# A fused graph kernel on Trainium2: the quotient of the mixing branch formed as 1 - eps/(v + eps)

## What is computed

```python
xn = _layernorm(x)
x = x + gnn(xn, edge_index) + mix(xn)      # graph attention, 8 heads of 32; mixing branch
x = x + ffn(_layernorm(x))                 # 8 gated experts, dense
```

```python
q = jax.nn.relu(q); k = jax.nn.relu(k)
vk  = jnp.einsum('ngdl,ngel->ngde', v, k)
out = jnp.einsum('ngde,ngdl->ngdl', vk, q)          # v * sum(k) * q here
out = out / (jnp.sum(v, -1, keepdims=True) + ATT_EPS)   # v itself here
```

## Time and profile before

| what | us |
|---|---|
| timed runs | 1016.85, 1018.16, 1018.79 |
| median | 1018.16 |
| profiled execution, span | 1012.8 |
| VectorE busy | 799.5 (79%) |
| TensorE busy | 911.4 (90%) |
| ScalarE busy | 589.4 (58%) |
| GpSimd busy | 377.3 (37%) |
| chain that ended last | TensorE 41%, GpSimd 34%, issue 13%, VectorE 7%, ScalarE 3%, DMA 2% |

### The profile page before, as it was taken

How to read it: one execution, slowest core, us unless ns; L and a number is a source line. 1 busy time by engine, 2 the same in 40 slices (tenths; PEclk the granted TensorE clock), 3 DMA queues, 4 the chain that set the end, 5 groups by cost and what they waited for, 6 DMA issues and landing times.

```text
span 1012.8 us, 14669 instructions
## 1 busy us (share of the span) xinstructions
PE 911.4 (90%) x4984; PEld 790.1 (78%) x4984; DVE 799.5 (79%) x1517; ACT 589.4 (58%) x1206; POOL 377.3 (37%) x408
## 2 busy tenths in 40 slices
PE   6897899989888999898746689999999999999997
PEld 5686788878777778777535578999988889898986
DVE  6778799988888888988786788775565778786867
ACT  4730456655656556666254566667665767666663
POOL 0167777777777777777773000000000000000000
PEclk9988899999999999998868799999999999999999
DMA  8434454454444444445563002000000010100013
GB/s 260 151 91 138 141 140 129 134 141 141 125 139 139 123 140 138 128 138 140 165 194 100 6 17 63 29 2 32 1 9 24 1 32 1 32 1 1 1 37 91
DMA packets 50362, 89.00 MB, mean 88 GB/s; under 512 B 9733, under 2 KB 33337, under 8 KB 50268
## 3 DMA queue, kind: packets, MB, share of 16 engines
q0 software_dynamic: 18768, 52.88, 19.0%
q1 hardware_dynamic: 30780, 34.66, 11.2%
q10 hardware_dynamic: 719, 0.27, 0.1%
HBM read 81.10 MB, written 6.68 MB: 87 GB/s over the span
## 4 chain that ended last, share of the span: by engine, by line
PE 41%; POOL 34%; issue 13%; DVE 7%; ACT 3%; DMA 2%; SPq 0%; POOLq 0%; DVEq 0%; ACTq 0%
POOL G L491 34%; PE bank L1043 9%; PE bank L1045 9%; PE bank L1044 9%; PE bank L1107 2%; PE bank L1110 2%; PE bank L837 2%; DMA x_in<-in_x 1%; PE bank L1108 1%; PE bank L1109 1%; PE bank L916 1%; ACT hid L741 1%; PE bank L872 1%; ACT sums L718 1%; PE bank L830 1%
## 5 line engine op out<-in xcount | busy, mean ns | idle before, releaser
L491 POOL DMA_INDIRECT G<-projected_rows,src_l x391 | 374.5, 958 | 166.6 <-issue 118.3
L741 ACT ACTIVATE hid<-bank,faff 128x512 f32<-128x512 f32 (+2 forms) x224 | 157.7, 723 | 111.1 <-PE bank L1045 109.3
L916 PE MATMUL bank<-G,oh 128*128 128x264 f32 x782 | 188.6, 400 | 21.3 <-DVE G L1422 21.1
L916 PEld LDWEIGHTS bank<-G,oh 128*128 128x128 f32 x782 | 153.5, 198 | 49.9 <-DVE G L1422 22.7
L1422 DVE TENSOR_TENSOR G<-G,bank 128x3072 f32<-128x3072 f32 (+1 forms) x33 | 109.1, 3306 | 0.0
L1716 DVE TENSOR_TENSOR hil<-hid,hil 128x1024 fp32r<-128x1024 f32 (+2 forms) x56 | 60.8, 1086 | 48.3 <-ACT hil L749 48.3
L1043 PE MATMUL bank<-frh,ew 128*128 128x512 f32 (+3 forms) x228 | 84.3, 370 | 4.4 <-DVE frl L1691 4.4
L1044 PE MATMUL bank<-frl,ew 128*128 128x512 f32 (+3 forms) x228 | 82.8, 363 | 0.0
L1045 PE MATMUL bank<-frh,ew 128*128 128x512 f32 (+3 forms) x228 | 82.8, 363 | 0.0
L1043 PE MATMUL bank<-hil,ew 128*128 128x512 f32 (+2 forms) x224 | 81.6, 364 | 0.0
L1045 PE MATMUL bank<-hil,ew 128*128 128x512 f32 (+2 forms) x224 | 81.2, 362 | 0.0
(11 more groups left out here) (344 smaller groups left out, 2059.3 us busy)
## 6 DMA issues: line engine op xcount, KB each, us to landing
dstb<-targets SPq DMA_DIRECT2D x32, 384.0 KB, 3.7
G<-projected_rows,src_l POOLq DMA_INDIRECT x391, 2.8
projected_rows<-sums SPq DMA_DIRECT2D x25, 132.0 KB, 2.2
x_in<-in_x SPq DMA_DIRECT2D x3, 1024.0 KB, 9.6
out<-feat_rows SPq DMA_DIRECT2D x23, 128.0 KB, 2.2
U<-in_x SPq DMA_DIRECT2D x4, 512.0 KB, 6.0
TT<-in_W SPq DMA_DIRECT2D x8, 256.0 KB, 3.3
wqkv<-in_W SPq DMA_DIRECT2D x8, 256.0 KB, 3.9
```

Source lines behind the costliest of these rows:

```text
L491: g.indirect_dma_start(out=G[slot][:, c, :], out_offset=None, in_=table[:, :], in_offset=bass.IndirectOffsetOnAxis(ap=src_l[:, grp, c:c + ...
L741: A.activation(hid[layer][:, m, 0:cols], bank[2 * layer + m][:, 0:cols], ACT.Relu, bias=faff[:, 2 * layer + 1, j:j + 1], scale=faff[:, 2 * ...
L916: ins = T.matmul(b_seg[g % 2][:, 0:ROW], oh[g % 2][:, c, :], G[g % SLOTS][:, c, :], start=(c == 0), stop=(c == ch - 1))
```

## The change

`ratio` forms v / (v + eps) as 1 - sign * (eps / |v + eps|). ScalarE gives eps / |v + eps| directly: ln(eps) is computed into a third column of `epsr` and is the bias of the exponential. VectorE keeps two instructions. `b_v` is no longer written.

```diff
-        epsr = [sb(f"epsr{i}", [P, 2]) for i in range(2)]
+        epsr = [sb(f"epsr{i}", [P, 4]) for i in range(2)]
...
                 chain.link(A.activation(e[:, 1:2], e[:, 0:1], ACT.Exp, scale=0.5, bias=lneps[:, 0:1]))
+                A.activation(e[:, 2:3], e[:, 1:2], ACT.Ln)
                 chain.link(A.activation(vbuf[t % 2], b_v[:, :], ACT.Abs, bias=e[:, 1:2]))
                 chain.link(A.activation(b_k[:, :], vbuf[t % 2], ACT.Ln))
-                A.activation(b_k[:, :], b_k[:, :], ACT.Exp, scale=-1.0)
+                A.activation(b_k[:, :], b_k[:, :], ACT.Exp, scale=-1.0, bias=e[:, 2:3])
...
                 par = t % 2
-                y = b_k[:, :]
                 dve.wait_ge(s["eps_ready"], t + 1)
-                link(V.tensor_tensor(b_v[:, :], b_v[:, :], kbuf[par], ALU.mult))
-                link(V.tensor_tensor(vbuf[par], vbuf[par], y, ALU.mult))
-                link(V.scalar_tensor_tensor(out=vbuf[par], in0=vbuf[par], scalar=-2.0, in1=y, op0=ALU.add, op1=ALU.mult))
-                link(V.tensor_tensor(b_v[:, :], vbuf[par], b_v[:, :], ALU.mult))
-                V.scalar_tensor_tensor(out=qbuf[par], in0=b_v[:, :], scalar=-1.0, in1=qbuf[par], op0=ALU.mult, op1=ALU.mult).then_inc(s["o_ready"], 1)
+                link(V.scalar_tensor_tensor(out=vbuf[par], in0=kbuf[par], scalar=-1.0, in1=b_k[:, :], op0=ALU.mult, op1=ALU.mult))
+                V.scalar_tensor_tensor(out=qbuf[par], in0=vbuf[par], scalar=1.0, in1=qbuf[par], op0=ALU.add, op1=ALU.mult).then_inc(s["o_ready"], 1)
```

## The result

| | before | after |
|---|---|---|
| timed runs, median of 8 each | 1017.69 us (1015.02 to 1018.79) | 1021.1 us (1019.17 to 1021.59) |
| ratio | | 1.0037, 95% interval [1.0026, 1.0048] |
| profiled execution, span | 1012.8 | 1018.5 |
| VectorE busy | 799.5 | 747.7 |
| gathers, busy (391) | 374.5 | 378.8 |

The change takes 52 us of work off VectorE and makes the kernel 3.4 us slower, by the medians. The prediction was 1021.4 (1018.16 + 3.3); the median of before has moved to 1017.69 with five more runs.

The account below looks back on a forecast made before the run. GpSimd's unpaused gathers were taken as the bound, so VectorE's saving counts nothing. Gathers held in 21 tiles at 0.157 us add 3.3 us to 1018.16, giving 1021.4 us, range 1017.2 to 1024.8.

Parts of the forecast that it names:

- The bound: From 133 to 485 us GpSimd's unpaused gathers set the time; VectorE's saved 49 us become waiting, 18.6 to about 68 us.
- VectorE's two instructions: In `ratio`, per tile: 0.72 us for the first with its link, 0.69 for the second, 1.41 instead of 3.59.
- ScalarE's 0.20 us: Ahead of VectorE's pair in each tile: added Ln 0.11 us, exponential's bias 0.09; VectorE starts 0.20 us later.
- The hold: A gather starting under the second, two-SBUF-input instruction lengthens by that instruction's end past its start less 0.125 us: about 0.16 us.
- The sum: Over 25 tiles, 21 held gathers at mean 0.157 us add 3.3 us to 1018.16, giving 1021.4 us.
- the one-hot excess: Gathers lengthened under one-input L1354: all such excess about 1 us in 133 to 485 us, its change taken as 0.
- 1 (the phase misses): In the tiles the second instruction ends too early to hold gathers much: 1018.2 to 1020.1 us, about 1019.6; 22%.
- 2 (only L1354's kind holds a gather): Two-SBUF-input instructions hold no gather; every gather under the new instruction keeps 0.95 us: 1018.2 us; 8%.
- 3 (VectorE paces the stage): VectorE, not GpSimd, bounds the tile stage, so its 49 us saving shows in the time: 969 us; 1%.
- 4 (a better clock at the end of the gathers): Group 31's sums and the dense stage's start run at a higher clock: 1016 us with no or little hold; 5%.
- 5 (a worse phase by ScalarE's part): ScalarE adds 0.33 us per tile, raising the hold to 6.0 us: 1024.2 us; 64% together with the forecast.
- 5.4 us between a span and a time: Whole kernel: the timed median lies 5.4 us above the profiled span, a distance kept for the forecast span of 1016.1 us.

Follow-up runs that it names:

- the second experiment: The changed kernel with one tiny linked VectorE instruction between the pair, so the second instruction runs 0.19 us later: 1.0069 of before, 1024.6 us.
- experiment 11: The changed kernel measured once more, unaltered, beside the kernel before: 1.0032 of before, 1020.89 us.
- Experiment 3: The changed kernel with three tiny linked VectorE instructions between the pair, so the second instruction runs 0.57 us later: 1.0024 of before, 1018.6 us.
- experiments 1, 4 and 5: 1: changed kernel, pair's intermediate result in PSUM, 1.0014 of before; 4: kernel before, L1546 with both inputs from SBUF, 1.0041; 5: kernel before, L1547 likewise, 1.0002.

## Why the prediction was right, point by point

- **The bound.** Gathers on GpSimd, with VectorE waiting for them: right. VectorE lost 52 us of work, and its wait rose to 69.2 us, "about 68" in the prediction.
- **VectorE's two instructions.** 0.72 to the second's start and 0.69 for it; measured 274.40 - 273.68 = 0.72, and 0.69. The working for the second was circular: its slope of 1 ns a column was drawn through L1544's own 687 ns, so it had to come out at 0.69. It assumed that both forms cost the same, and they do.
- **ScalarE's 0.20 us.** The Ln 0.11, as estimated; the bias 0.08 (0.58 us for this exponential before, 0.66 after). VectorE's wait for Sign rose from 0.18 to 0.36, so 0.18 in all.
- **The hold.** 0.29 us of overlap past the start expected, 0.25 to 0.29 measured in 22 tiles; 0.16 us each expected, 0.12 to 0.16 measured. The formula (end past the start, less 0.125 us), read from three rows, held in all of them: 0.28 past the start at 274.81 gives 0.16, and the gather has 1.10. It held at other phases too: 0.58 to 0.59 in the first tile (0.46; the gather has 1.41), 0.44 in the second experiment (0.32; it has 1.26).
- **The sum.** 21 tiles and 3.3 us expected; 23 tiles and 3.7 us in the trace, 3.4 us in the time. The first tile had 0.46, where the largest term expected was 0.26. The gathers' total rose by 4.3, since the one-hot excess rose by 0.6 as well, which the prediction had put at 0. It had taken all excess of the kernel before in 133 to 485 us for about 1 us, and the trace has 1.7. That the forecast of 1021.4 lies only 0.3 us from the measured median is partly luck: the median of before moved by 0.5 us, and by the ratio the loss is 3.8 us here and 3.3 in experiment 11.
- **The rivals.** 1 (the phase misses) did not come: two tiles missed, not all. Experiment 3 made it happen, and 1.0024 was left, the 2 us that are open. 2 (only L1354's kind holds a gather) is refuted by experiments 1, 4 and 5. This was also what the inference in the Trainium skill ("SBUF — State Buffer", section "Who interferes with whom") came to; it does not hold for these gathers, the fourth experiment's tensor_tensor being the plainest case. The first half of that rule, that a two-input instruction contends with GpSimd instructions that read SBUF, would fit: the gather takes its row numbers from src_l, which lies in SBUF. That this read is what waits was not tried. 3 (VectorE paces the stage) did not come: 52 us less of its work, and the time rose. 4 (a better clock at the end of the gathers) did not either: the sums of group 31 take 8.03 us at a granted clock of 0.69, against 7.98 at 0.70 before, and what follows the last gather is as long, 468.6 against 468.5. They were in part at a lower clock, but the 24 pieces are two products a chunk, not one. 5 (a worse phase by ScalarE's part) did not come: 0.18 us, not 0.33.
- **One reading was wrong.** The prediction kept 5.4 us between a span and a time. In the executions that give both, the distance is 2.0 us (median), and the executions of before beside the experiments have a median span of 1014.4 to 1014.8: the profiled one with its 1012.8 was a quick one. As only the difference counted, the sum did not suffer, but the spans must not be compared as if they were medians: they differ by 5.7 us, 0.9 of which is the first gather's later start (its wait for stored rows is 44.2 against 43.3 us), ahead of anything changed.

## What to carry to other kernels

When GpSimd issues indirect gathers without a pause and they are the bound, look for VectorE instructions with two SBUF inputs that lie over the start of a gather: here each was paid for, whatever VectorE's idle time. Routing one input through PSUM removed the hold. For the pair it cost nothing in duration (0.69 us either way); for the one-hot instruction, as another operation, it cost 1.1 us. Before an instruction list is shortened, look at which memory each remaining operand comes from: here five instructions, each with a PSUM input, were free, and two, one of them without, cost 3.4 us. Work moved by a few tenths of a microsecond against such a rhythm can gain or lose as much as the work itself.

## What the runs showed of the hardware

- A gather that starts while a VectorE instruction with two SBUF inputs runs takes longer by the distance from its start to the instruction's end, less 0.125 us: 0.16 us at 0.28, 0.32 at 0.44, 0.46 at 0.59. Only the start is sensitive: instructions that began 0.07 us (the change's third tile) or 0.16 us (experiment 3) after the gather's start cost nothing.
- With one input in PSUM the same instruction at the same place costs nothing (0.942 to 0.948 us against 1.06 to 1.11), and neither does one of 1.75 us. Of 89 gathers that start under L1422 (3.3 us, one input in PSUM) in the kernel before, none is held.
- A one-input tensor_scalar of 128x1536 from int16 to bf16, all in SBUF, takes 0.61 us and holds a gather's start in the same way. It holds it at a second place too: begun 0.22 to 0.49 us behind the start, it lengthens the gather by its end less 0.83 us (0.18 us at 1.01). As tensor_tensor with a PSUM column it takes 1.75 us and does neither. One SBUF input alone is not enough: under the tensor_reduce L1534 four gathers start in the kernel before, and none is held.
- A bias column adds 0.08 us to ScalarE's exponential of 128x512: 0.58 us in the kernel before, 0.66 in the change. For one column an exponential with a bias takes 0.29 us and a logarithm without one 0.20.
